# Halo matmuls paired inside a pair of chunks instead of with the pair before, in a four-image convolution kernel

## The chip, the cores and the metric

One core of a Trainium2 chip. The metric is device microseconds of one launch; a kernel before the change is run three times, and the median is given. One further execution was taken by the hardware profiler; all rows below are of that one. PE is TensorE's matmul part, DVE VectorE, ACT ScalarE, POOL GpSimd, SP the sync engine, which here only issues DMAs.

## The reference

```python
x = x + conv3x3(group_norm(x), L0_weight) + L0_bias
x = x + conv3x3(group_norm(x), L1_weight) + L1_bias
x = x + experts(group_norm(x))    # 8 experts: gelu(x w1 + b1) w2 + b2
x = x + conv3x3(group_norm(x), L3_weight) + L3_bias
```

x is (4, 8, 256, 256) in float32. A group is two of the eight channels of one image, so an image has to be complete before its next layer can be normalised. The experts are matrices over the width (256 to 1024 to 256), one per channel.

## The kernel before, in words

x stays in SBUF through all layers. A partition holds one of 8 channels, one of 8 neighbouring rows and one of the two columns of a column pair; an image is 32 x 128 = 4096 columns in 8 chunks of 512 (`CH`). A convolution layer is four steps, one per image: steps 0 to 3 are L0, 4 to 7 are L1, 8 to 11 are L3, with the experts between 7 and 8. A step treats its chunks in four pairs; "(g, k)" is pair k of step g.

Every number is used as a sum of two float16 parts, high and low, and three products of parts are accumulated (`PRODUCTS`). A step's way through the engines:
- statistics: DVE's `stats_chunk` per chunk (L586) and `aggregate` (L591); PE's `group_mean` (L807) and `group_variance` (L812), between them DVE's `deviation` and after them `variance`; GpSimd's `scale_and_bias` (L344 to L351) gives `norm_ok`.
- normalised input: ACT writes the high part in XN (L448) and the full value in SCR (L454), two buffers of two chunks; GpSimd subtracts (L365, `low_part`). In step 0 the full value is made by DVE instead (`first_whole`, L651, in PRE) and ACT writes only high parts.
- halos: rows above and below lie in other partitions. SP copies them by DMA from XN to HALO (L256), eight DMAs for the first half of the image (`halo_a`, after the third low part, or in step 0 the fourth) and eight for the second (`halo_b`).
- PE, per chunk, in one PSUM bank: three 128x128 matmuls (`centre`, L833), three times two 64x64 ones (`sides`, L840 and L842: the neighbouring columns), three times two 49x64 ones (`halo`, L852 and L854: rows and bias). The two of `sides` and the two of `halo` take the four quarters of the array, and run at once if they belong to different chunks. `sides` and `halo` of the same chunk write the same bank, and are kept apart by a wait.
- DVE adds the bank to x (`conv_update`, L624) and takes the next statistics from it (L586); in steps 8 to 11 there are no next statistics.

The order around the change is written out by hand in each engine's block. `tiles(pair, behind)` issues the sides of pair k beside the halos of pair k-1. So the first call of steps 0 and 8 has sides alone, a last call after steps 7 and 11 halos alone, and a pair is complete one call after its sides. PE waits for `halo_a` or `halo_b` before a call with halos of that half, and for `side_mm`, which a pair's last sides raised one call earlier. Five PSUM banks serve as a ring (`RING`): the centre of chunk q waits for the update of chunk q-5. GpSimd's list of `low_parts`, `scale_and_bias` and `pre_chunk` (input of the experts, transposed by PE, L892, split by ACT and DVE, L478 and L633) is a fixed sequence; `PREPARED` gives the steps in which transposes are made. In steps 0 and 1 PE and DVE also take the statistics of images 1 to 3 and of step 0's result in between.

SP's queue is in order: x (image 0 in four pieces), the ones (bias rows of HALO), the halos of steps 0 to 7, the expert weights, the halos of steps 8 to 11. Before the halos of step 10 and again before those of step 11 it waits for the image of step 8, or of step 9, and stores it (2 MB); image 2 and the eight chunks of image 3 are stored behind the halos of step 11.

## Time and profile before

| what | us |
|---|---|
| three runs | 606.98, 607.93, 610.66 (median 607.93) |
| the profiled execution, its own time | 608.81 |
| its span (first to last instruction) | 607.0 |
| PE busy in the span | 532.9 |
| DVE, ACT, POOL busy | 382.4, 266.7, 159.5 |
| experts in PE's timeline, about | 169 to 530 |

Busy PE is the time in which a matmul is in flight; back to back they overlap, so it is not PE at its peak. The stretches matter more than the totals: steps 0 to 7 lie before 169 us, steps 8 to 11 after 540 us. Statistics of the idle time name the instruction that came last before the engine went on.

### The profile page before, as it was taken

The numbers are of one execution on the slowest core, as the hardware profiler recorded it, in microseconds if no ns is written. First come the engines' busy times: TensorE is split into PE (matmuls) and PEld (weight loads), VectorE is DVE, ScalarE is ACT, GpSimd is POOL, SyncE is SP. The second block draws the span as 40 slices with busy tenths as digits, with TensorE's granted clock in tenths as the row PEclk, the third lists the DMA queues.
The fourth block names the chain that finished last, engine by engine and source line by source line (L and its number), as shares of the span: only waits on it lengthen the run. The fifth ranks groups of instructions, "written<-read, shape, count | busy, mean of one in ns | idle before, by whom it ended". The sixth has DMA issues, their size and how long they took to land.

```text
span 607.0 us, 9074 instructions
## 1 busy us (share of the span) xinstructions
PE 532.9 (88%) x3312; PEld 252.0 (42%) x3312; DVE 382.4 (63%) x658; ACT 266.7 (44%) x311; POOL 159.5 (26%) x168
## 2 busy tenths in 40 slices
PE   1565697999888999999999999999999997878984
PEld 0321242445454544444444444444444454544431
DVE  4996485999987549339158085193491638788533
ACT  0366348772353545336145163352461543665510
POOL 3744366997436000000000000000000000566520
PEclk9997797999979999999999999999999998979998
DMA  8724035554231022110120111011100000034678
GB/s 338 284 75 102 26 88 137 127 141 107 75 129 70 1 70 70 70 30 39 69 69 9 60 69 69 0 69 69 65 4 1 0 1 1 23 82 104 209 246 305
DMA packets 12293, 53.18 MB, mean 88 GB/s; under 512 B 2908, under 2 KB 3036, under 8 KB 9308
## 3 DMA queue, kind: packets, MB, share of 16 engines
q1 hardware_dynamic: 11976, 52.22, 26.7%
q10 hardware_dynamic: 288, 0.57, 0.3%
q8 instruction: 19, 0.31, 0.2%
q14 instruction: 10, 0.08, 0.0%
HBM read 25.83 MB, written 8.39 MB: 56 GB/s over the span
## 4 chain that ended last, share of the span: by engine, by line
PE 63%; DVE 21%; POOL 6%; SPq 3%; issue 2%; DMA 2%; ACT 1%; POOLq 0%; ACTq 0%; DVEq 0%
PE PS L952 27%; PE PS L931 25%; DVE ST L586 9%; PE PS L833 4%; POOL XN L365 4%; DVE X L624 4%; PE PS L840 3%; SPq L256 3%; DVE X L640 2%; DVE XT L633 2%; DVE PRE L651 1%; PE PS L908 1%; DMA X<-x 1%; PE PS L892 1%; DVE HID L724 1%
## 5 line engine op out<-in xcount | busy, mean ns | idle before, releaser
L931 PE MATMUL PS<-XT,W1S 128*128 (+1 forms) x768 | 171.8, 382 | 3.9 <-DVE W1S L647 3.7
L952 PE MATMUL PS<-HID,W2S 128*128 128x512 f16 x768 | 171.0, 380 | 1.6 <-DVE W2S L647 1.6
L486 ACT ACTIVATE SCR<-PS,CONST 128x512 f32<-128x512 f32 x128 | 87.3, 688 | 73.2 <-PE PS L931 37.1
L931 PEld LDWEIGHTS PS<-XT,W1S 128*128 128x128 f16 x768 | 75.5, 99 | 93.1 <-issue 7.0
L952 PEld LDWEIGHTS PS<-HID,W2S 128*128 128x128 f16 x768 | 75.4, 99 | 88.5 <-issue 2.4
L724 DVE SCALAR_TENSOR_TENSOR HID<-SCR,HID 128x512 f16<-128x512 f32 x128 | 88.5, 691 | 14.1 <-ACT HID L507 10.0
L365 POOL TENSOR_TENSOR XN<-SCR,XN 128x1024 f16<-128x1024 f32 x44 | 90.4, 2070 | 18.9 <-ACT SCR L454 18.6
L586 DVE BATCH_NORM_STATS2 ST<-X 128x6 f32<-128x512 f32 x128 | 86.3, 690 | 10.7 <-DMA X<-x 7.3
L647 DVE SCALAR_TENSOR_TENSOR W2S<-W2F,W2S 128x2048 f16<-128x2048 f32 x8 | 18.3, 2292 | 118.6 <-ACT W2S L482 118.6
L448 ACT ACTIVATE XN<-X,SC 128x1024 f16<-128x1024 f32 (+1 forms) x49 | 59.1, 1214 | 75.0 <-POOL SC L351 75.0
L624 DVE SCALAR_TENSOR_TENSOR X<-PS,X 128x512 f32<-128x512 f32 x96 | 64.9, 679 | 42.1 <-PE PS L854 41.7
L833 PE MATMUL PS<-XN,CWT 128*128 128x512 f16 x288 | 78.3, 408 | 12.7 <-DMA HALO<-ones 7.3
L333 POOL MEMSET HALO<- 48x520 f16 x12 | 6.3, 526 | 311.8 <-PE PS L931 311.2
L840 PE MATMUL PS<-XN,CWT 64*64 64x512 f16 x288 | 74.8, 395 | 5.6 <-DMA HALO<-XN 5.6
L842 PE MATMUL PS<-XN,CWT 64*64 64x512 f16 x288 | 74.8, 395 | 0.0
L852 PE MATMUL PS<-HALO,CWT 49*64 49x512 f16 (+1 forms) x288 | 73.5, 388 | 0.2 <-PE PS L842 0.2
L854 PE MATMUL PS<-HALO,CWT 49*64 49x512 f16 (+1 forms) x288 | 73.5, 388 | 0.0
L521 ACT ACTIVATE YT<-PS,CONST 128x512 f32 (+1 forms) x32 | 22.0, 687 | 114.0 <-PE PS L952 114.0
L454 ACT ACTIVATE SCR<-X,SC 128x1024 f32<-128x1024 f32 x44 | 54.0, 1228 | 15.6 <-POOL XN L365 15.6
L721 DVE TENSOR_SCALAR HID<-SCR 128x512 f16<-128x512 f32 x120 | 50.7, 422 | 8.5 <-ACT SCR L486 4.9
L833 PEld LDWEIGHTS PS<-XN,CWT 128*128 128x128 f16 x288 | 27.1, 106 | 51.3 <-issue 22.8
L840 PEld LDWEIGHTS PS<-XN,CWT 64*64 64x64 f16 x288 | 28.1, 111 | 47.1 <-issue 22.7
(43 smaller groups left out, 401.5 us busy)
## 6 DMA issues: line engine op xcount, KB each, us to landing
W1F<-w SPq DMA_DIRECT2D x8, 1024.0 KB, 4.8
W2F<-w SPq DMA_DIRECT2D x8, 1024.0 KB, 4.8
HALO<-XN SPq DMA_DIRECT2D x48, 129.9 KB
out<-X SPq DMA_DIRECT2D x3, 2048.0 KB, 7.0
HALO<-XN SPq DMA_DIRECT2D x48, 121.8 KB
X<-x SPq DMA_DIRECT2D x2, 2048.0 KB, 18.9
HALO<-XN SPq DMA_DIRECT2D x48, 64.9 KB
HALO<-XN SPq DMA_DIRECT2D x48, 60.9 KB
```

What stands on the lines that cost most here:

```text
L365: pool.tensor_tensor(XN[s][:, 1, rows, 1:NJ + 1], whole, XN[s][:, 0, rows, 1:NJ + 1], ALU.subtract).then_inc(lo_ok, 1)
L486: act.activation(SCR[:, ft % 2, 0:CH], bank(ft % G_RING), ACT.Gelu, bias=BT[:, ds(e * FT + ft, 1)], scale=1.0 / (XS * WS)).then_inc(gelu_o ...
L586: dve.bn_stats(ST[:, n % 4, slot], src).then_inc(bn_ok, 1)
L624: dve.scalar_tensor_tensor(out=xc, in0=bank(conv_bank(q)), scalar=1.0 / (XS * WS), in1=xc, op0=ALU.mult, op1=ALU.add).then_inc(x_new, 1)
L724: dve.scalar_tensor_tensor(out=HID[p][:, 1, ft], in0=SCR[:, ft % 2, 0:CH], scalar=HS, in1=HID[p][:, 0, ft], op0=ALU.mult, op1=ALU.subtract ...
L833: pe.matmul(to, CWT[:, w, l, 0:P], XN[s][:, part, rows, 1:NJ + 1], start=(n == 0), stop=False)
L840: odd = pe.matmul(bank(k, HALF_P, P), CWT[0:HALF_P, w, l, SIDE:EDGE], XN[s][0:HALF_P, part, rows, 2:NJ + 2], start=False, stop=False)
L842: even = pe.matmul(bank(k, 0, HALF_P), CWT[HALF_P:P, w, l, SIDE:EDGE], XN[s][HALF_P:P, part, rows, 0:NJ], start=False, stop=False)
L852: even = pe.matmul(bank(k, 0, HALF_P), CWT[0:kh, w, l, EDGE:CWN], HALO[s][0:kh, part, rows, 0:NJ], start=False, stop=last)
L854: odd = pe.matmul(bank(k, HALF_P, P), CWT[HALF_P:HALF_P + kh, w, l, EDGE:CWN], HALO[s][HALF_P:HALF_P + kh, part, rows, 0:NJ], start=False, ...
L931: mm = pe.matmul(bank(ft % G_RING), W1S[:, w, h * NF + ft * P:h * NF + (ft + 1) * P], rhs, start=(n == 0), stop=(n == 3 * DH - 1))
L952: mm = pe.matmul(bank(G2_BANK + h), W2S[:, w, ft * NW + h * P:ft * NW + (h + 1) * P], HID[p][:, part, ft], start=(ft == 0 and part == 0 an ...
```

## The change

Eight edits, all in the order of the work; the arithmetic stays.
1. `tiles(g, k)` treats one pair (a, b): sides of a beside halos of b, then a wait for all four of the last matmuls (`cross_mm`), then sides of b beside halos of a. There is no call with sides or halos alone. Both chunks of a pair end together, and `conv_update` waits for both. PE waits for the pair's halos at once.
2. Step 0's full-precision copy moves from DVE to ACT, by way of SCR, as in other steps.
3. GpSimd's list becomes regular: all low parts of a step but the last, then the next `scale_and_bias`, then the last; `pre_chunk` 0 comes behind all low parts of step 7.
4. Stores of images 0 to 2 leave SP's queue for ACT's, in halves: image 0 after the second and fourth normalised piece of step 11, images 1 and 2 behind that. SP keeps the eight chunks of image 3.
5. Image 0 is loaded in pieces of 3, 2, 2 and 1 chunks instead of four times two.
6. `deviation` and `variance` of steps 2 to 7 come one pair later on DVE; on PE, statistics 2 one pair earlier.
7. XT's low parts are made by DVE behind the pair of the same number instead of one pair earlier.
8. A slot of XN is free when the whole step has been computed (`conv_mm`), not when its sides have.

```diff
+X0_CUTS = (0, 3, 5, 7, 8)
...
 for _g in range(8, 12):
     for _k in range(NPR):
...
-        if (_g, _k) != (8, 0):
-            _q = NCH * _g + 2 * _k - 2
-            ORDER += [("c", _q // NCH, _q % NCH), ("c", _q // NCH, _q % NCH + 1)]
-ORDER += [("c", 11, NCH - 2), ("c", 11, NCH - 1)]
+        ORDER += [("c", _g, 2 * _k), ("c", _g, 2 * _k + 1)]
...
-            load_image(0, k * NT // 4, (k + 1) * NT // 4, x0_in[k])
+            load_image(0, TC * X0_CUTS[k], TC * X0_CUTS[k + 1], x0_in[k])
...
             halos(g)
-            if g >= 9:
-                sp.wait_ge(x_new, X_NEW_AT["c", g - 1, NCH - 1])
-                store_image(g - 9, 0, NT)
...
         def pre_chunk(m):
-            if m == 0:
-                pool.wait_ge(lo_ok, FIRST_PIECE[1])
...
-        low_parts(0)
-        scale_and_bias(1)
-        low_parts(1, 0, 3)
-        scale_and_bias(2)
-        low_parts(1, 3)
-        low_parts(2, 0, 2)
-        scale_and_bias(3)
-        low_parts(2, 2)
-        scale_and_bias(4)
-        low_parts(3)
...
-        scale_and_bias(8)
-        pre_chunk(0)
-        pre_chunk(1)
-        low_parts(7, 3)
-        for j in range(2, NCH):
+        for g in range(8):
+            low_parts(g, 0, -1)
+            scale_and_bias(g + 1)
+            low_parts(g, -1)
+        for j in range(NCH):
             pre_chunk(j)
...
-            if g > 0:
-                if m >= FIRST_PIECE[1] + 2:
-                    act.wait_ge(lo_ok, m - 1)
-                act.activation(SCR[:, m % 2, 0:n * CH], src, ACT.Identity,
+            if m >= 2:
+                act.wait_ge(lo_ok, m - 1)
+            act.activation(SCR[:, m % 2, 0:n * CH], src, ACT.Identity,
...
-                act.wait_ge(side_mm, 2 * NPR * (f + 1))
+                act.wait_ge(conv_mm, 2 * NCH * (f + 1))
...
+        def store_half(b, i):
+            act.wait_ge(x_new, X_NEW_AT["c", 8 + b, i + NCH // 2 - 1])
+            act.dma_start(out[b][:, i * CH:(i + NCH // 2) * CH], x_chunk(b, i, NCH // 2)
+                          ).then_inc(out_done, 16)
...
+        slot_free(11)
+        for k in range(NPR):
+            normalise_piece(FIRST_PIECE[11] + k)
+            if k % 2:
+                store_half(0, NPR * (k // 2))
+        for b in range(1, NB - 1):
+            for i in range(0, NCH, NCH // 2):
+                store_half(b, i)
...
-            dve.wait_ge(conv_mm, 2 * (q + 1))
+            dve.wait_ge(conv_mm, 4 * (q // 2 + 1))
...
-        dve.wait_ge(norm_ok, 1)
-        for i in range(NCH):
-            first_whole(i)
...
-                if i == 1 and g >= 2:
+                if i == 3 and g >= 2:
                     deviation(3 + g)
-                if i == 3 and g >= 2:
+                if i == 5 and g >= 2:
                     variance(3 + g)
-
-                after = (g, (i + 1) // 2) if i < NCH - 1 else (g + 1, 0)
-                if i % 2 and after in PREPARED:
-                    for m in PREPARED[after]:
+                if i % 2 and (g, i // 2) in PREPARED:
+                    for m in PREPARED[g, i // 2]:
                         xt_low(m)
...
+        def tiles(g, k):
+            a, b = 2 * k, 2 * k + 1
+            arrived = halo_a if 2 * k < SPLIT else halo_b
+            pe.wait_ge(arrived[SLOT[g]], HALO_HALF * (USES[g] + 1))
+            for n, (part, w) in enumerate(PRODUCTS):
+                first = cross_mm if n == 2 else None
+                sides(g, a, part, w, first)
+                halo(g, b, part, w, first)
+
+            pe.wait_ge(cross_mm, 4 * (NPR * g + k + 1))
+            for n, (part, w) in enumerate(PRODUCTS):
+                second = conv_mm if n == 2 else None
+                sides(g, b, part, w, second)
+                halo(g, a, part, w, second)
...
-                q = NPR * g + k - 1
-                tiles((g, k), (q // NPR, q % NPR) if q >= 0 else None)
+                tiles(g, k)
+                if g == 0 and k == 1:
+                    group_mean(2)
                 if g == 0 and k == 2:
-                    group_mean(2)
-                if g == 0 and k == 3:
                     group_variance(2)
...
-        tiles(None, (7, NPR - 1))
```

## Rows read from the trace of the kernel before

**Rows 1.** Busy time by stretch: us of each engine (instructions), granted clock, DMA share, GB/s.
```profile
112.00:137.00 25.00, 23.99 (x244) 10.38 (x240) 24.23 (x47) 20.52 (x19) 24.12 (x21) 1.00 0.53 133
...
565.00:607.00 42.00, 32.35 (x341) 13.06 (x339) 17.03 (x29) 9.17 (x8) 9.65 (x8) 0.96 0.78 275
```

**Rows 2.** Timeline of PE, 25 to 27 us: start, us, what [idle before, releaser].
```profile
25.75 1.86 PE L833 MATMUL PS<-XN,CWT 128*128 128x512 f16 x4 [7.34 <-DMA HALO<-ones]
```

**Rows 3.** Timeline of VectorE, 16 to 27 us.
```profile
17.40 8.94 DVE L651 TENSOR_SCALAR PRE<-X,SC 128x512 f32<-128x512 f32 x8 [0.90 <-POOL SC L351]
```

**Rows 4.** Timeline of VectorE, 30 to 46 us.
```profile
32.55 0.14 DVE L597 TENSOR_TENSOR SM<-MV,PS 128x1 f32<-128x1 f32 x1
...
37.04 0.63 DVE L624 SCALAR_TENSOR_TENSOR X<-PS,X 128x512 f32<-128x512 f32 x1
```

**Rows 5.** Timeline of PE, 47 to 58 us.
```profile
53.47 0.59 PE L807 MATMUL PS<-MV,CONST 128*128 128x1 f32 x2 [5.05 <-DVE MV L591]
```

**Rows 6.** Timeline of VectorE, 57 to 81 us.
```profile
58.08 0.69 DVE L624 SCALAR_TENSOR_TENSOR X<-PS,X 128x512 f32<-128x512 f32 x1 [4.43 <-PE PS L854]
...
72.38 0.69 DVE L624 SCALAR_TENSOR_TENSOR X<-PS,X 128x512 f32<-128x512 f32 x1 [4.14 <-PE PS L854]
...
80.90 0.37 DVE L591 BATCH_NORM_AGGREGATE MV<-ST 128x2 f32<-128x48 f32 x1
```

**Rows 7.** Timeline of PE, 94 to 100 us.
```profile
96.15 0.63 PE L840 MATMUL PS<-XN,CWT 64*64 64x512 f16 x1 [3.68 <-DMA HALO<-XN]
```

**Rows 8.** Timeline of GpSimd, 77 to 97 us.
```profile
81.07 0.55 POOL L344 TENSOR_TENSOR RS<-SM,RS 128x1 f32<-128x1 f32 x1 [7.06 <-DVE SM L609]
```

**Rows 9.** Timeline of SP's queue, 530 to 607 us: start, us, DMA issues.
```profile
580.34 14.22 SPq L256 DMA_DIRECT2D HALO<-XN  x16
594.60 9.56 SPq L240 DMA_DIRECT2D out<-X  x9
```

**Rows 10.** Chain that ended last, 580 to 607 us: start, us, what.
```profile
580.99 1.38 SPq L256
...
587.32 0.62 SPq L256
...
593.93 2.36 DMA HALO<-XN
...
598.88 1.34 DVE X L624 x2
```

**Rows 11.** Timeline of PE, 584 to 588.5 us.
```profile
584.26 1.49 PE L833 MATMUL PS<-XN,CWT 128*128 128x512 f16 x6
...
587.11 1.49 PE L833 MATMUL PS<-XN,CWT 128*128 128x512 f16 x6
```

**Rows 12.** Timeline of PE, 597 to 600 us.
```profile
597.45 0.38 PE L852 MATMUL PS<-HALO,CWT 49*64 49x512 f16 x1
...
598.00 0.37 PE L852 MATMUL PS<-HALO,CWT 49*64 49x512 f16 x1 [0.17 <-PE PS L842]
...
598.21 0.38 PE L852 MATMUL PS<-HALO,CWT 48*64 48x512 f16 x1
```

**Rows 13.** Page, part 5: costliest groups (x count, busy us, mean ns, idle before, releaser).
```profile
L365 POOL TENSOR_TENSOR XN<-SCR,XN 128x1024 f16<-128x1024 f32 x44 | 90.4, 2070 | 18.9 <-ACT SCR L454 18.6
...
L454 ACT ACTIVATE SCR<-X,SC 128x1024 f32<-128x1024 f32 x44 | 54.0, 1228 | 15.6 <-POOL XN L365 15.6
```

**Rows 14.** Timeline of PE, 164 to 170 us.
```profile
168.81 1.44 PE L931 MATMUL PS<-XT,W1S 128*128 128x512 f16 x3 [3.73 <-DVE W1S L647]
```

**Rows 15.** Timeline of VectorE, 164 to 175 us.
```profile
166.42 2.28 DVE L647 SCALAR_TENSOR_TENSOR W1S<-W1F,W1S 128x2048 f16<-128x2048 f32 x1
...
171.39 0.37 DVE L591 BATCH_NORM_AGGREGATE MV<-ST 128x2 f32<-128x48 f32 x1
```

**Rows 16.** Timeline of GpSimd, 565 to 582 us.
```profile
569.71 0.19 POOL L351 TENSOR_TENSOR SC<-SM,SC 128x1 f32<-128x1 f32 x1
```

**Rows 17.** Page, part 6: DMA issues: x count, KB each, median us to landing.
```profile
out<-X SPq DMA_DIRECT2D x3, 2048.0 KB, 7.0
```

More of the change, by code:

```diff
@@ L356, in low_part @@
             s = SLOT[g]
+            pool.wait_ge(xn_ok, m + 1)
             pool.wait_ge(hi_ok, m + 1)
-            if g == 0:
-                pool.wait_ge(whole0_ok, i + n)
-                whole = whole0[:, i:i + n].rearrange("p c (t j) -> p (c t) j", j=NJ)
-            else:
-                pool.wait_ge(xn_ok, m + 1 - FIRST_PIECE[1])
-                whole = SCR[:, m % 2, 0:n * CH].rearrange("p (t j) -> p t j", j=NJ)
             rows = slice(i * TC, (i + n) * TC)
-            pool.tensor_tensor(XN[s][:, 1, rows, 1:NJ + 1], whole,
+            pool.tensor_tensor(XN[s][:, 1, rows, 1:NJ + 1],
+                               SCR[:, m % 2, 0:n * CH].rearrange("p (t j) -> p t j", j=NJ),
                                XN[s][:, 0, rows, 1:NJ + 1], ALU.subtract).then_inc(lo_ok, 1)
@@ L577, in _ @@
         normalise_piece(FIRST_PIECE[8] + 3)
-        for g in range(9, 12):
-            normalise(g)
+        def store_half(b, i):
+            act.wait_ge(x_new, X_NEW_AT["c", 8 + b, i + NCH // 2 - 1])
+            act.dma_start(out[b][:, i * CH:(i + NCH // 2) * CH], x_chunk(b, i, NCH // 2)
+                          ).then_inc(out_done, 16)
+        for g in range(9, 11):
+            normalise(g)
+        slot_free(11)
[6 more added lines that the diff above has]
+                store_half(b, i)
     @block.vector
@@ L613, in input_stats @@
             if b == 0:
-                dve.wait_ge(x0_in[i // 2], 16)
+                if i in X0_CUTS:
+                    dve.wait_ge(x0_in[X0_CUTS.index(i)], 16)
             elif b == 1:
@@ L834, in centre, with sides, halo @@
                           start=(n == 0), stop=False)
-        def sides(g, i, part, w, last):
+        def sides(g, i, part, w, signal=None):
             s, l, k = SLOT[g], g // 4, conv_bank(NCH * g + i)
-            rows = slice(i * TC, (i + 1) * TC)
+            rows, last = slice(i * TC, (i + 1) * TC), signal is conv_mm
             odd = pe.matmul(bank(k, HALF_P, P), CWT[0:HALF_P, w, l, SIDE:EDGE],
-                            XN[s][0:HALF_P, part, rows, 2:NJ + 2], start=False, stop=False)
+                            XN[s][0:HALF_P, part, rows, 2:NJ + 2], start=False, stop=last)
             even = pe.matmul(bank(k, 0, HALF_P), CWT[HALF_P:P, w, l, SIDE:EDGE],
-                             XN[s][HALF_P:P, part, rows, 0:NJ], start=False, stop=False)
-            if last:
-                even.then_inc(side_mm, 1)
-                odd.then_inc(side_mm, 1)
-        def halo(g, i, part, w, last):
+                             XN[s][HALF_P:P, part, rows, 0:NJ], start=False, stop=last)
+            if signal is not None:
+                even.then_inc(signal, 1)
+                odd.then_inc(signal, 1)
+        def halo(g, i, part, w, signal=None):
             s, l, k = SLOT[g], g // 4, conv_bank(NCH * g + i)
-            rows, kh = slice(i * TC, (i + 1) * TC), KH if part == 0 else HK
+            rows, last = slice(i * TC, (i + 1) * TC), signal is conv_mm
+            kh = KH if part == 0 else HK
             even = pe.matmul(bank(k, 0, HALF_P), CWT[0:kh, w, l, EDGE:CWN],
@@ L856, in halo @@
                             start=False, stop=last)
-            if last:
-                even.then_inc(conv_mm, 1)
-                odd.then_inc(conv_mm, 1)
-        def tiles(pair, behind):
-            for c in range(2):
-                if behind is not None and c == 0:
-                    g, k = behind
-                    arrived = halo_a if 2 * k < SPLIT else halo_b
-                    pe.wait_ge(arrived[SLOT[g]], HALO_HALF * (USES[g] + 1))
-                    pe.wait_ge(side_mm, 2 * (NPR * g + k + 1))
-                for n, (part, w) in enumerate(PRODUCTS):
-                    if pair is not None:
-                        g, k = pair
-                        sides(g, 2 * k + c, part, w, n == 2 and c == 1)
-                    if behind is not None:
-                        g, k = behind
-                        halo(g, 2 * k + c, part, w, n == 2)
+            if signal is not None:
+                even.then_inc(signal, 1)
+                odd.then_inc(signal, 1)
+        def tiles(g, k):
[11 more added lines that the diff above has]
+                halo(g, a, part, w, second)
         def before_step(g):
@@ L1068, in _ @@
                     group_variance(15)
-                q = NPR * (g - 8) + k - 1
-                tiles((g, k), (8 + q // NPR, q % NPR) if q >= 0 else None)
-        tiles(None, (11, NPR - 1))
+                tiles(g, k)
     ctx.close()
```

32 lines of the change are left out of this document (6 added, 26 removed).

## The prediction, made before the changed kernel was run

> **What bounds the kernel now.** The busy time by stretch comes first. Between 112 and 137 us PE is busy for 23.99 of 25 us and VectorE for 24.23, at full clock: steps 4 and 5 are a tie. From 565 us PE has 32.35 of 42 us, with DMA busy for 0.78 of it [rows 1]. Experts (169 to 530 us) aren't touched. So three places can move: the front, the pace of the conv steps, and the tail.
>
> The front: PE's first matmul waits until 25.75 for the ones, which lie in SP's queue behind all of x [rows 2]. VectorE meanwhile makes step 0's full-precision copy for 8.94 us [rows 3]. It reads mean 1 at 32.55 and starts its first update at 37.04 [rows 4]. In step 1 PE and VectorE alternate instead of overlapping: PE idles 5.05 us for statistics 3 [rows 5], VectorE 4.43 and 4.14 us for PE (and 4.20 and 2.62 in the same view), 15.4 us in all; step 1 ends at 81.27 [rows 6]. In step 3 PE waits 3.68 us for a halo and restarts at the lower clock [rows 7]; the cause is GpSimd, which stood 7.06 us at scale 4, with step 3's low parts behind it [rows 8].
>
> The tail: SP issues step 11's halo copies from 580.34 to 594.56, and only then image 2's store and image 3's eight chunks, nine issues in 9.56 us [rows 9]. The chain runs through these copies, a landing of 2.36 us, PE and two updates [rows 10].
>
> All starts are of the profiled execution: span 607.0, time 608.81, so 1.8 us lie around it; the median of the three runs is 607.93, 0.88 below.
>
> **Part 1: the pairing.** A pair costs six centre and six side/halo starts: centres begin at 584.26 and again at 587.11, a pitch of 2.85 us [rows 11]. The new tiles have the same six starts, but PE must see the first three finish before the fourth. This drain exists once now, in the tail: a start at 597.45, the next at 598.00 [rows 12], 0.55 apart, against 0.21 to the one after that. That is 0.34 more; four signals rather than two are awaited, so I take 0.36 a pair (below: 0.15, if the array drains anyway at each change from centres to tiles; above: 0.5). A pair becomes 3.21 us, a step with its two statistics (0.2 each) 13.2 us. VectorE needs 12.2 with its waits in steps 4 and 5, so PE becomes the bound. Behind the wait stand the second half, the next centres and statistics; VectorE waits for all of it, and now gets both chunks at once.
> The Trainium skill (TensorE: Matmul & The Clock Gate, The cost: per-tile semaphore tail) says that increments on tiles serialize, 26.3 ns each; by it two more awaited cost 0.05 us a pair, an estimate from that page, 1.8 us over the 35 drains that matter.
>
> **Part 2: nothing lags.** No sides go in front and no halos behind: 1.5 us less of PE at 163.6 and at 598.0, but there the gain is given back: at the end VectorE's two updates (1.34 us, [rows 10]) no longer overlap the last halos. In step 1 VectorE has pair (1,0) complete before it ends step 0, so the alternation goes. The cost is that tiles (0,0), hence everything behind it on PE, now waits for halo_a(0).
>
> **Part 3: the front, step by step.** The copies move from VectorE to ScalarE. Norm 0 still comes at 17.4 (three chunks land first, at about 7.5, and eight stats then take until 12.4 as now). A copy takes ScalarE 1.23 us per two chunks and its other pass as much, GpSimd's low part takes 2.07 [rows 13]; ScalarE paces, with a piece every 2.27 us in its timeline. The fourth low part ends at 27.1 (26.0 now), SP issues eight halos of 0.65 us until 32.4, they land 2.4 after the last issue starts: tiles (0,0) run 34.4 to 37.3, at the lower clock (1.2 GHz, as after the idle time in [rows 7], where starts are 0.43 apart) since PE idles six us before. Centres to 39.0, then mean 1. VectorE, which freed 8.9 us, stands at deviation 1 from about 23 until 39.4 and its gain is lost. Norm 1 comes at 43.0, and the first update at 44.1, 7.1 us late.
> GpSimd now does step 0's last low part behind scale 1: 45.1; its eight halos land at 52.2; tiles (0,2) end at 55.1, where VectorE (at 52.2) waits 2.9. Step 0's statistics end at 63.7 (53.6 now). Scale 2, then low part (1,3), then halos: 70.0, so tiles (1,2) end at 71.8 (VectorE waits 2.1). Step 1 ends at 78.3, and tiles (2,0) at 78.7, against 81.5 now for the same work: **2.8 us ahead**, because 15.4 us of alternation shrink to some 2.
>
> **Part 4: steps 2 to 7.** Scale 4 no longer stands in front of step 3's first three low parts: 80.4, halos landed at 87.4, needed at 90.2. So [rows 7] goes: 3.7 idle plus about 2.6 at the lower clock, 6.3 us. Next late would be GpSimd, at 4 x 2.27 + 1.9 = 11.0 a step, under 13.2. From (2,1) to (7,3) are 23 drains: +8.3. Pre chunk 0 now comes behind all of step 7's low parts, PE waits 1.3 for it (0.6 now); a second small wait (0.65) goes, with 1.0 of transposes in front of the last halos and 0.7 of other gaps. The deviations and variances come one pair later (3 us); cover: step 4's halos land at 98.0 and are needed at 103.3, later steps have as much, and without it each us late stands on PE. The wait for a free slot on the whole step instead of its sides ends at the same matmuls. Sum: 83.6 us now (81.5 to 165.1) - 6.3 + 8.3 + 0.7 - 2.35 = 84.0. Tiles (7,3) end at about 162.8.
> At present W1's low part stands in front of the last two updates, and PE starts the experts at 168.81 [rows 14], while VectorE still updates until 171.6 [rows 15]. After the change the last updates (2.65) and two XT parts (1.2) come between: W1 ends at 164.8, 167.5, 168.7. The experts start at 168.7: **0.1 us earlier**. Three gains of 2.8, 6.3 and 3.1 us end in nothing, by the drains and this order.
>
> **Part 5: tail.** In step 8 VectorE need not wait as now at the ring: tiles (9,0) end at 563.7 with pair (9,0) complete, 3.5 us ahead. Norm 15 depends on (9,3)'s update and comes at 570.8 (569.9 now, [rows 16]). Seven pairs of 3.21 and one statistic later, (11,0) could start at 588.3. SP, without stores, starts halos 11 at 580.0 rather than 580.34: the low parts bind, not SP. Eight issues at 0.65 (if nothing slows them; 1.38 and 0.62 both stand in [rows 10]) and the landing give 587.6, and the second half 592.9 for a need at 594.7.
> Stores now go from ScalarE: image 0 in halves after pieces 1 and 3 of step 11 (the issue, some 0.4 us, moves pieces 2 and 3 and the low parts behind them), image 1 at once behind, image 2 at 582 and 588. So some 5 MB are in flight from 580 on, beside the halos. A store of 2 MB takes 7.0 us [rows 17], so the backlog lasts to about 598. For both together I allow the halos 1.2 us (bounds: 0.4, the issue alone, and rival 1). PE ends at 600.8 (599.5 now), the updates at 602.1 (600.2), the last store is issued at once rather than behind eight others, and lands about 2.9 later (3.6 for the last now, behind a full queue), 605.0; the exit 0.4. Span 605.4, less the 0.1: **605.3**, 1.7 us less than 607.0. The time is 607.1 for that execution, 606.2 for the median.
> The Trainium skill (DMA: Bandwidth & Descriptors, Issuing engines are not separate DMA queues) says that DMAs of all engines share the same 16 engines, so issuing from another one saves only the issuing time. By it the move saves SP's nine issues and not the contention; the 4 slow issues in [rows 10] agree that a store slows halos, but no row here has the store on another queue.
>
> **Rivals.** 1 (slower): ScalarE's stores hold up halos 11. Now a store of 2 MB makes four of the copies behind it last 1.38 instead of 0.62. With 5 MB in flight some 14 of 16 would: the second half lands at 580.0 + 14 x 1.42 + 1.3 + 2.4 = 603.6, then two pairs less a centre run (4.9), updates 1.3, store 3.3: span 613.1, time 614.0. It decides from the fifth slow copy on. For it: [rows 10]. Against it: they shared one queue, and PE in step 10 didn't wait. 0.17.
> 2 (faster): the drain is mostly there already, 0.15 a pair. 35 x 0.21 = 7.4 us less (a step is then 12.4, still over VectorE's 12.2): 598.8. For it: 12 x 0.21 is 2.55, so the pitch of 2.85 already holds 0.3 for its two changes of shape [rows 11, 12]. Against it: [rows 12], where the same mechanism shows its 0.55. 0.18.
> 3: the waits at the front don't add as worked out: mean 1 late by 7 us pushes statistics 2 and 3 and all behind them, and halos in steps 2 and 3 come late again. 3 to 5 us more, 610. 0.15. In itself within 1%.
> Forecast: 0.50.
>
> **Numbers.** A measurement tells from no change about 1%, 6.1 us: below 601.9 faster, above 614.0 slower. Slower has most of rival 1 and the end of rival 3: 0.17. Faster has rival 2 and little else: 0.18. The rest 0.65. The range reaches to rival 2's 598.8 and to rival 1's 614.0; it leaves out 0.2.
>
> **Signs.** Right, if the first update stands at about 44, VectorE's alternation in step 1 shrinks to under 4 us, no halo wait stands at step 3, the pitch of a pair is 3.2 us, halos 11 are issued in about 10.5 us, and one or two stores follow the last update. Wrong, if the pitch is under 3.05 or over 3.35, if many copies of step 11 last 1.3 or more, or if the first update starts before 40.

## The result, and the profile after

The changed kernel takes 615.00 us (median of 4 runs, 614.41 to 615.68) against 608.64 us for the kernel before in the same comparison: a ratio of 1.0103 with a 95% interval of 1.0069 to 1.0138. It is slower by 1.0%, where 606.2 us was forecast, with 614.0 as the upper end. The profiled execution took 614.91 us with a span of 613.1, against a forecast span of 605.3.

First the page of the kernel after: span, busy time by engine, DMA by fortieth of the span, one group and one row of DMA issues.

```profile
span 613.1 us, 9025 instructions
...
PE 536.8 (88%) x3312; PEld 245.7 (40%) x3312; DVE 372.7 (61%) x650; ACT 271.3 (44%) x316; POOL 159.2 (26%) x168
...
DMA  8613455542211021110111021102100000224784
...
L806 PE MATMUL PS<-XN,CWT 64*64 64x512 f16 x288 | 83.8, 399 | 27.4 <-DMA HALO<-XN 20.3
...
out<-X ACTq DMA_DIRECT2D x6, 1024.0 KB, 7.1
```

Of the 27.4 us for which PE stands in front of tiles, 20.3 are put down to halo copies. Three waits make up most of them: 5.08 and 5.58 us in step 0, and one of 9.01 in the tail. The busy time by stretch shows that one from above (the columns are those of [rows 1]):

```profile
565.00:579.00 14.00, 13.28 (x141) 4.53 (x144) 5.29 (x10) 8.93 (x8) 7.43 (x7) 1.00 0.64 207
579.00:593.00 14.00, 8.04 (x78) 2.62 (x70) 3.87 (x6) 0.24 (x1) 2.19 (x2) 0.99 0.99 369
593.00:599.00 6.00, 2.51 (x24) 0.74 (x24) 0.00 (x0) 0.00 (x0) 0.00 (x0) 0.50 0.60 175
599.00:613.00 14.00, 9.66 (x98) 3.11 (x90) 5.16 (x8) 0.00 (x0) 0.00 (x0) 0.98 0.42 154
```

To 579 us PE is busy for 13.28 of 14 us. From 579 to 593 it has 8.04 of 14, and the DMA engines are busy for 0.99 of the time at 369 GB/s: that stretch belongs to them. The third row has a granted clock of 0.50, so PE restarts at 1.2 GHz. The chain of waits names what stood in front (start, us, what):

```profile
579.64 0.16 SPq L247
...
579.85 1.38 SPq L247
581.27 1.40 SPq L247
582.71 2.06 SPq L247
584.80 1.96 SPq L247
586.80 2.14 SPq L247
588.98 2.28 SPq L247
591.31 4.99 DMA HALO<-XN
...
596.34 0.63 PE PS L806
```

L247 is SP issuing step 11's halo copies. The second to the eighth last 1.38 to 2.28 us (1.41 the eighth, which began at 591.31), and the copies land at 596.30, 4.99 us after the last of them was begun. In the kernel before, four copies of 1.37 to 1.40 us stand behind the store [rows 10], the others take 0.59 to 0.63 but for one of 1.32 at 591.90, and the landing takes 2.36. On ScalarE's queue stand the stores beside which they ran (start, us, engine, line, operation):

```profile
576.88 1.82 ACTq L545 DMA_DIRECT2D out<-X  x3
...
580.98 6.72 ACTq L545 DMA_DIRECT2D out<-X  x2
```

A first half image had gone at 570.08 and landed at 574.93. Three more (3 MB) are issued at 576.88, 577.27 and 577.76, a further one at 580.98 and the last at 587.36. The one of 577.76 lands at 588.44 and the one of 580.98 at 591.74, 10.7 and 10.8 us after their issue, where a whole image took 7.0 [rows 17]. So five half images, 5 MB, are under way at some time beside the copies, but never more than 3 MB of them at once.

PE's timeline in the kernel after: where it begins the experts, one pair of step 9 and the next centres, and the restart in the tail:

```profile
169.60 1.01 PE L897 MATMUL PS<-XT,W1S 128*128 128x512 f16 x2 [5.01 <-DVE XT L612]
...
566.71 1.49 PE L799 MATMUL PS<-XN,CWT 128*128 128x512 f16 x6
568.13 0.40 PE L806 MATMUL PS<-XN,CWT 64*64 64x512 f16 x1
...
569.12 0.40 PE L806 MATMUL PS<-XN,CWT 64*64 64x512 f16 x1
...
569.90 1.49 PE L799 MATMUL PS<-XN,CWT 128*128 128x512 f16 x6
...
596.34 0.63 PE L806 MATMUL PS<-XN,CWT 64*64 64x512 f16 x1 [9.01 <-DMA HALO<-XN]
```

Centres to centres is 569.90 - 566.71 = 3.19 us (2.85 in [rows 11]). The drain, PE's wait until the first half of a pair's tiles is finished, lies between the two groups: the first group's third starts come at 568.59, the next group's first at 569.12, 0.53 later against 0.21 inside a group. PE starts the experts at 169.60, where [rows 14] have 168.81. Around 203 us the two kernels stand level again (203.02 and 203.11), so the front gave and took nothing on balance. VectorE at the front:

```profile
37.99 0.15 DVE L575 TENSOR_TENSOR SM<-MV,PS 128x1 f32<-128x1 f32 x1 [16.23 <-PE PS L773]
...
42.49 0.63 DVE L603 SCALAR_TENSOR_TENSOR X<-PS,X 128x512 f32<-128x512 f32 x1
```

It stands 16.23 us at deviation 1 and makes its first update at 42.49 (37.04 in [rows 4]).

### The profile page after: what moved, and what is told of

It is laid out like the page before. It is cut to its first block, busy times and chain, and to the rows that moved or that the text cites. A ratio compares the mean times of both kernels' runs of the same rounds, so it can differ in the third digit from the quotient of the medians.

```text
span 613.1 us, 9025 instructions
## 1 busy us (share of the span) xinstructions
PE 536.8 (88%) x3312; PEld 245.7 (40%) x3312; DVE 372.7 (61%) x650; ACT 271.3 (44%) x316; POOL 159.2 (26%) x168
## 4 chain that ended last, share of the span: by engine, by line
PE 73%; DVE 11%; SPq 4%; POOL 3%; DMA 3%; ACT 3%; issue 2%; DVEq 0%; POOLq 0%; ACTq 0%
PE PS L918 27%; PE PS L897 25%; PE PS L806 9%; PE PS L799 7%; DVE ST L564 4%; SPq L247 4%; DMA HALO<-XN 2%; DVE X L603 2%; DVE X L619 2%; PE PS L858 2%; PE PS L874 1%; POOL XN L349 1%; DMA X<-x 1%; ACT XN L413 1%; ACT SCR L418 1%
## 5 line engine op out<-in xcount | busy, mean ns | idle before, releaser
L450 ACT ACTIVATE SCR<-PS,CONST 128x512 f32<-128x512 f32 x128 | 87.2, 687 | 72.4 <-PE PS L897 36.3
L806 PE MATMUL PS<-XN,CWT 64*64 64x512 f16 x288 | 83.8, 399 | 27.4 <-DMA HALO<-XN 20.3
L349 POOL TENSOR_TENSOR XN<-SCR,XN 128x1024 f16<-128x1024 f32 (+1 forms) x49 | 99.4, 2030 | 25.1 <-ACT SCR L418 25.1
L819 PE MATMUL PS<-HALO,CWT 49*64 49x512 f16 (+1 forms) x288 | 84.2, 400 | 0.0
L821 PE MATMUL PS<-HALO,CWT 49*64 49x512 f16 (+1 forms) x288 | 84.2, 400 | 0.0
L808 PE MATMUL PS<-XN,CWT 64*64 64x512 f16 x288 | 83.8, 399 | 0.0
L799 PE MATMUL PS<-XN,CWT 128*128 128x512 f16 x288 | 75.1, 399 | 8.1 <-DMA HALO<-ones 8.1
L418 ACT ACTIVATE SCR<-X,SC 128x1024 f32<-128x1024 f32 (+1 forms) x49 | 59.3, 1210 | 0.0
L806 PEld LDWEIGHTS PS<-XN,CWT 64*64 64x64 f16 x288 | 23.8, 108 | 81.9 <-PE PS L821 31.5
L799 PEld LDWEIGHTS PS<-XN,CWT 128*128 128x128 f16 x288 | 27.1, 105 | 45.1 <-issue 22.7
```

The lines of the kernel that those rows point to most:

```text
L349: pool.tensor_tensor(XN[s][:, 1, rows, 1:NJ + 1], SCR[:, m % 2, 0:n * CH].rearrange("p (t j) -> p t j", j=NJ), XN[s][:, 0, rows, 1:NJ + 1] ...
L450: act.activation(SCR[:, ft % 2, 0:CH], bank(ft % G_RING), ACT.Gelu, bias=BT[:, ds(e * FT + ft, 1)], scale=1.0 / (XS * WS)).then_inc(gelu_o ...
L799: pe.matmul(to, CWT[:, w, l, 0:P], XN[s][:, part, rows, 1:NJ + 1], start=(n == 0), stop=False)
L806: odd = pe.matmul(bank(k, HALF_P, P), CWT[0:HALF_P, w, l, SIDE:EDGE], XN[s][0:HALF_P, part, rows, 2:NJ + 2], start=False, stop=last)
L808: even = pe.matmul(bank(k, 0, HALF_P), CWT[HALF_P:P, w, l, SIDE:EDGE], XN[s][HALF_P:P, part, rows, 0:NJ], start=False, stop=last)
L819: even = pe.matmul(bank(k, 0, HALF_P), CWT[0:kh, w, l, EDGE:CWN], HALO[s][0:kh, part, rows, 0:NJ], start=False, stop=last)
```

## The experiments

All ratios are against the kernel before, on the same chip. The kernel after was timed only in the first comparison, where the kernel before had 608.64 us; in the three later ones it had 607.83 to 608.10. Differences to the 615.00 us therefore cross two comparisons. My theory after the result: the bytes of the stores that are in flight beside step 11's halo copies cost the time, and the rest of the change is neutral. Rivals: the drains cost it and the stores only show it; ScalarE's queue is what hurts, not the bytes; the late start of the front costs it.

**e1: after, with images 0 to 2 stored by SP behind step g's halos again.**

```diff
             halos(g)
+            if g >= 9:
+                sp.wait_ge(x_new, X_NEW_AT["c", g - 1, NCH - 1])
+                sp.dma_start(out[g - 9], x_chunk(g - 9, 0, NCH)).then_inc(out_done, 16)
...
-        for g in range(9, 11):
+        for g in range(9, 12):
             normalise(g)
-        slot_free(11)
-        for k in range(NPR):
-            normalise_piece(FIRST_PIECE[11] + k)
-            if k % 2:
-                store_half(0, NPR * (k // 2))
-        for b in range(1, NB - 1):
-            for i in range(0, NCH, NCH // 2):
-                store_half(b, i)
```

> The changed kernel with one part undone: images 0 to 2 are stored from SP's queue again, as before the change (each whole, after the halos of the next step but one). Theory S (ScalarE's stores slow the halo copies of step 11, PE waits 9.0 us for them): the wait before tiles (11,0) shrinks to under 4 us, at most five of the sixteen copies last over 1 us, and the time is 606 to 609 us, against 615.0. Theory D (the drains alone are the loss): the copies don't matter to the end, 614 to 615 us.

Measured: 607.21 us, ratio 0.9987 (0.9970 to 1.0005), span 605.5. Every copy of step 11 lasts 0.59 to 0.69 us, the second half's issues end at 591.5, no wait stands at tiles (11,0), and the last update ends at 601.8. The busy time of the stretch in which the kernel after stood:

```profile
579.00:593.00 14.00, 13.41 (x135) 4.38 (x132) 5.65 (x9) 1.97 (x2) 3.92 (x2) 1.00 0.72 232
```

PE has 13.41 of 14 us instead of 8.04. So 7.8 us of the kernel after (7.1 by the two ratios, 7.6 by the spans) are the stores' place alone, and everything else that the change does comes to no measurable difference. (Its last update ends 1.6 us later than in the kernel before, and 3.7 us of the span are left behind it instead of 6.8.) Image 1's store went out at 576.67 and landed at 583.60, and the copies, from 580.94, were not slowed by the rest of it: a store begun 4.3 us ahead of them cost nothing, where the one begun 0.6 us ahead (579.72, kernel before) cost four slow copies.

**e2: before, with only the stores moved to ScalarE in halves**, as the kernel after has them.

```diff
             halos(g)
-            if g >= 9:
-                sp.wait_ge(x_new, X_NEW_AT["c", g - 1, NCH - 1])
-                store_image(g - 9, 0, NT)
...
-        for g in range(9, 12):
+        for g in range(9, 11):
             normalise(g)
+        slot_free(11)
+        for k in range(NPR):
+            normalise_piece(FIRST_PIECE[11] + k)
+            if k % 2:
+                store_half(0, NPR * (k // 2))
+        for b in range(1, NB - 1):
+            for i in range(0, NCH, NCH // 2):
+                store_half(b, i)
```

> The kernel before with the changed kernel's stores of images 0 to 2 on ScalarE's queue, all else as before. Theory S: step 11's copies slow down here too (six or more over 1.3 us), the first half lands at about 596 rather than 590.5, and since PE needs it one pair later and has 2 us of slack at the end of the queue, the time rises by only 1 to 3 us over the kernel before. Rival: the slow copies belong to the new pairing's timing; then SP's freed queue makes this kernel 2 to 4 us faster than before.

Measured: 611.47 us, ratio 1.0055 (1.0037 to 1.0073), span 609.2. Seven copies of step 11 last 1.19 to 2.49 us, and PE waits 7.87 us at 595.3. PE's timeline has it:

```profile
595.29 0.63 PE L850 MATMUL PS<-XN,CWT 64*64 64x512 f16 x1 [7.87 <-DMA HALO<-XN]
```

It is the same wait in the other order of the work, so it belongs to the stores and not to the pairing. The last update ends at 606.7, 6.5 us later than in the kernel before (600.2). The time grows by only 3.4 (1 to 3 were expected), since the move also gives something back: of the old span 6.8 us lie behind the last update, where SP's nine issues stand [rows 9], and here 2.5.

**e3: before, with the drain alone**, a wait for the first half of each group of sides and halos.

```diff
+    half_mm = sem("half_mm")
...
+                if c == 1 and pair is not None:
+                    g, k = pair
+                    pe.wait_ge(half_mm, 2 * (NPR * g + k + 1))
                 for n, (part, w) in enumerate(PRODUCTS):
...
-                        sides(g, 2 * k + c, part, w, n == 2 and c == 1)
+                        sides(g, 2 * k + c, part, w, n == 2 and c == 1,
+                              half_mm if n == 2 and c == 0 else None)
```

> The kernel before with a drain added in the middle of each pair's tiles (PE waits for the third group's side matmuls before it starts the fourth), same matmuls in the same order. Theory D: pitch of a pair 3.19 instead of 2.85 us in steps 4 and 5, the experts start 4 to 6 us later, the whole is 5 to 9 us slower. Rival (VectorE's 12.2 us a step covers it): under 2 us slower.

Measured: 607.89 us, ratio 1.0004 (0.9977 to 1.0031). A miss: 5 to 9 us were expected and none came. The drain is there, in PE's timeline:

```profile
106.67 0.40 PE L841 MATMUL PS<-XN,CWT 64*64 64x512 f16 x1
...
107.59 0.40 PE L841 MATMUL PS<-XN,CWT 64*64 64x512 f16 x1
...
108.37 1.49 PE L834 MATMUL PS<-XN,CWT 128*128 128x512 f16 x6
109.79 0.40 PE L841 MATMUL PS<-XN,CWT 64*64 64x512 f16 x1
```

A pair takes 109.79 - 106.67 = 3.12 us, 0.27 over [rows 11]. But where PE then waits for something else, the drain is paid out of that wait: the halo wait of step 3 is 2.86 instead of 3.68, and step 3 ends at 109.7 instead of 110.9. In the tail a wait of 1.89 us at 590.5 is gone too. Steps 4 and 5, the tie of [rows 1], do lengthen (12.9 and 13.2 us against 12.2 and 11.9), and the experts start 0.7 us later, at 169.5. A cost per pair times the number of pairs is an upper bound on the end time, not an estimate of it.

**e4: after, with mean and variance 1 ahead of tiles (0,0).**

```diff
-                if (g, k) == (0, 1):
+                if (g, k) == (0, 0):
                     group_mean(1)
                     group_variance(1)
```

> The changed kernel with mean 1 and variance 1 issued on PE ahead of tiles (0,0) instead of behind them. Theory F (VectorE's 16 us wait at deviation 1, 21.8 to 38.0, throws away what it gained in the front): VectorE's first update stands at 36 to 37 instead of 42.5, halo_b(0) no longer waits for norm 1, tiles (2,0) start at 66 to 68 instead of 76.1, and the experts start some 9 us earlier: 605 to 608 us. Rival (another wait takes over, as GpSimd's order or statistics 3 and 4): 611 to 615.

Measured: 608.1 us, ratio 0.9994 (0.9977 to 1.0011), 6.9 us under the kernel after (6.6 by the ratios). VectorE at the front:

```profile
28.40 0.15 DVE L575 TENSOR_TENSOR SM<-MV,PS 128x1 f32<-128x1 f32 x1 [6.58 <-PE PS L773]
...
36.59 0.69 DVE L603 SCALAR_TENSOR_TENSOR X<-PS,X 128x512 f32<-128x512 f32 x1 [3.60 <-PE PS L821]
```

The wait shrinks from 16.23 to 6.58 us and the first update comes at 36.59, 5.9 us sooner. PE starts the experts at 161.6, 8.0 us sooner than in the kernel after. Then the tail takes some back: eight slow copies, and PE waits 9.33 us at 588.9. So the front's late start is real and costs 8 us at the experts. Since the two kernels stand level around 203 us all the same, the rest of the new order must have earned as much. PE starts the experts 8 us sooner here where some 9 were expected.

**e5: after, ScalarE's half stores kept apart from step 11's copies**: image 0 ahead of step 11's pieces, image 1 at 571.7 and 576.2, image 2 when halo_b of step 11 has landed.

```diff
+        store_half(0, 0)
+        store_half(0, NPR)
         slot_free(11)
+        store_half(1, 0)
         for k in range(NPR):
             normalise_piece(FIRST_PIECE[11] + k)
-            if k % 2:
-                store_half(0, NPR * (k // 2))
...
+            if k == 1:
+                store_half(1, NPR)
+        act.wait_ge(halo_b[SLOT[11]], HALO_HALF * (USES[11] + 1))
+        store_half(2, 0)
+        store_half(2, NPR)
```

> The changed kernel, still with six half stores on ScalarE's queue, but placed apart from the halos of step 11: image 0 after step 10's pieces (about 562), image 1 before piece 0 and after piece 1 of step 11 (570 and 575), image 2 only when the second half of step 11's halos has landed. Theory S: the first copies of step 11 are issued at 0.62 us but for two or three behind image 1, PE's wait before (11,0) is under 3 us, 605 to 609 us. If the queue that issues is what slows the copies and not the bytes in flight, 5 or more stay over 1 us and the time stays at 612 or more.

Measured: 608.90 us, ratio 1.0011 (0.9996 to 1.0026). There is one slow copy (1.29 us), no wait at tiles (11,0), and the last update ends at 601.8. With the same queue and the same sizes at other times the loss is gone. It is the overlap that costs, not the issuing engine.

**e6: after, with the next pair's centres between the two halves of the tiles**, to fill the drain.

```diff
...
-                tiles(g, k)
+                tiles_first(g, k)
+                centres(g, k + 1)
...
+                tiles_second(g, k)
```

> The changed kernel with the same pairing, but the centres of the next pair stand between the two halves of a pair's tiles, so that PE has 1.4 us of work while the first half finishes. Theory D: the 0.55 us between the two halves goes, pitch 2.85 to 2.95 us, VectorE's 12.2 us bind steps 2 to 5, experts start 4 to 6 us earlier; step 11 still waits for its halos, so only that carries to the end: 609 to 612 us. If the ring of five banks holds the centres (they need the update of the pair that has just ended), pitch stays over 3.1 and the time at 614 to 616.

Measured: 624.64 us, ratio 1.0271 (1.0245 to 1.0296). A miss, and a large one: 9.6 us slower than the kernel after. The drain is gone from PE's timeline: in step 10, which has no statistics and no wait, a step takes 11.4 us (4 x 2.85) where the kernel after has 12.8. But elsewhere the time isn't: the second half of a pair now comes behind the next pair's centres, so VectorE gets both chunks later, and PE waits for VectorE at the statistics. One such place, VectorE's timeline:

```profile
116.87 0.14 DVE L575 TENSOR_TENSOR SM<-MV,PS 128x1 f32<-128x1 f32 x1
...
117.11 1.44 DVE L579 SCALAR_TENSOR_TENSOR SM<-SM,MV 128x1 f32<-128x1 f32 x1
...
122.09 0.69 DVE L603 SCALAR_TENSOR_TENSOR X<-PS,X 128x512 f32<-128x512 f32 x1 [0.77 <-PE PS L821]
```

and PE's waits (in total, times, longest):

```profile
PE PS L806 <- DMA HALO<-XN: 23.8, 4, 11.9
...
PE PS L778 <- DVE SM L579: 10.6, 9, 1.9
```

In the kernel after the second sum is 5.5. By the ends of the steps, step 1 takes 20.1 us (14.8 in the kernel after) and step 2 16.6 (13.7); steps 3 and 4 give 2.0 back, and step 5 takes 13.6 in both. The experts start at 174.8 instead of 169.6, 5.2 us later; by the end of step 10 it is 8.0 (595.3, not 587.3), and PE's wait for step 11's halos is 11.9 us instead of 9.0. That the later second half is what starts the waits is argued from these rows; no run has it by itself.

**e7: after, with images 0 to 2 held until step 11's last halo has landed.**

```diff
...
-        slot_free(11)
...
+        act.wait_ge(halo_b[SLOT[11]], HALO_HALF * (USES[11] + 1))
-        for b in range(1, NB - 1):
+        for b in range(NB - 1):
             for i in range(0, NCH, NCH // 2):
                 store_half(b, i)
```

> The changed kernel with all stores of images 0 to 2 held until the last halo copy of step 11 has landed. A measurement of the copies without any store: theory S says all sixteen last 0.59 to 0.64 us from 579.2 on, the first half lands at about 587, PE doesn't wait at (11,0), and PE ends at 600 instead of 609. The end is then bound by 8 MB of stores from about 593 on: span 611 to 616. If the copies are slow for another reason, PE's wait stays.

Measured: 618.49 us, ratio 1.0167 (1.0145 to 1.0189). The copies last 0.59 to 0.63 us but for one of 1.03, PE doesn't wait and the last update ends at 602.4 (601.8 in e1). But then the stores are what is left:

```profile
585.00:600.00 15.00, 14.38 (x140) 4.83 (x138) 6.44 (x10) 0.00 (x0) 0.00 (x0) 1.00 0.76 258
600.00:616.00 16.00, 0.85 (x12) 0.26 (x12) 1.29 (x2) 0.00 (x0) 0.00 (x0) 0.60 0.90 361
```

Sixteen microseconds at 361 GB/s with PE done. The stores must be early or in between; both ends cost.

**e8: e4's, e5's and e6's edits together**, with mean and variance 1 in front of step 0's first tiles.

```diff
...
+        centres(0, 0)
+        group_mean(1)
+        group_variance(1)
...
+                tiles_first(g, k)
+                centres(g, k + 1)
+                tiles_second(g, k)
...
+        act.wait_ge(halo_b[SLOT[11]], HALO_HALF * (USES[11] + 1))
+        store_half(2, 0)
+        store_half(2, NPR)
```

> The changed kernel with the three edits together: mean 1 and variance 1 ahead of tiles (0,0), next centres between the halves, stores apart from the halos. If the three causes are separate, the gains add: 615 less 9 (front), 5 (drains before the experts), 8 (stores), 3 (drains in the tail), 588 to 596 us, faster than both kernels. If one hides behind another, 600 or more.

Measured: 605.03 us (603.10 to 609.38, a wide scatter), ratio 0.9963 (0.9934 to 0.9992). Again a miss: e6's order, which I had expected to gain 8 us, takes back some 5 to 7 of what the two others give (compare e9 below, 598.00 without it). It starts the experts at 165.8 where e4 had 161.6, and 13.4 us of PE's waits are for deviations (5.5 in the kernel after). By this and e6 the drain is better left where it is in steps that have statistics; in step 10, which has none, filling it gains 1.4 us in both.

**e9: after, with e4's and e1's edits** (mean and variance 1 ahead of tiles (0,0); images 0 to 2 on SP).

```diff
-                if (g, k) == (0, 1):
+                if (g, k) == (0, 0):
...
+            if g >= 9:
+                sp.wait_ge(x_new, X_NEW_AT["c", g - 1, NCH - 1])
+                sp.dma_start(out[g - 9], x_chunk(g - 9, 0, NCH)).then_inc(out_done, 16)
...
```

> The changed kernel with two edits: mean 1 and variance 1 ahead of tiles (0,0), as in e4, and the stores of images 0 to 2 back on SP's queue, as in e1. If both costs are separate: experts start at 161.6 as in e4, step 10 ends at 580, no wait over 3 us before (11,0), and 599 to 602 us, faster than both kernels by 1%. If the front's gain is lost again in the tail: 605 or more.

Measured: **598.00 us** (597.76 to 598.61, 5 runs), ratio 0.9837 (0.9824 to 0.9850). It beats both kernels, the one before by 1.6%. The stretches of the tail:

```profile
565.00:579.00 14.00, 13.42 (x136) 4.56 (x129) 5.76 (x9) 6.59 (x6) 8.15 (x4) 1.00 0.73 247
579.00:593.00 14.00, 11.44 (x118) 3.72 (x115) 5.83 (x10) 0.00 (x0) 0.00 (x0) 1.00 0.87 315
```

No wait stands at tiles (11,0), PE is busy until its work ends (the last update ends at 592.4), the experts start at 161.6, no copy lasts over 1 us. What e4 gains at the front, 8 us, arrives at the end in full once the tail doesn't give it back (607.2 in e1, 598.0 here). The time is 1 us below the 599 to 602 expected.

**e10: after, with only image 1 (2 MB) beside step 11's copies, still on ScalarE's queue.**

```diff
...
+        store_half(0, 0)
+        store_half(0, NPR)
+        normalise(11)
+        store_half(1, 0)
+        store_half(1, NPR)
+        act.wait_ge(halo_b[SLOT[11]], HALO_HALF * (USES[11] + 1))
+        store_half(2, 0)
+        store_half(2, NPR)
```

> The changed kernel with only 2 MB (image 1) on ScalarE's queue beside the first halo copies of step 11, at the same moment as in the changed kernel (577); image 0 goes at 562, image 2 after the last halo has landed. Theory S-bytes (the copies wait for the bytes in flight, whatever the queue): four, at most five copies over 1 us, as with 2 MB on SP's queue in the kernel before; PE waits 2 to 4 us before (11,0); 607 to 610 us. Theory S-queue (a second queue is what hurts): seven copies slow as in the changed kernel, 613 or more.

Measured: 609.16 us, ratio 1.0026 (1.0003 to 1.0048). Its chain of waits:

```profile
580.37 1.39 SPq L247
...
581.80 1.44 SPq L247
...
583.29 1.18 SPq L247
...
584.51 1.06 SPq L247
...
585.61 0.59 SPq L247
...
586.91 2.43 DMA HALO<-XN
```

There are four slow copies, as many as the kernel before has behind an image on SP's own queue, and the landing is back at 2.43 us. PE waits 1.51 us, less than the 2 to 4 expected.

**e11: after, all stores on SP, with images 0 and 1 (4 MB) right ahead of step 11's copies.**

```diff
+            if g == 11:
+                sp.wait_ge(x_new, X_NEW_AT["c", 9, NCH - 1])
+                sp.wait_ge(lo_ok, PIECE_OF[11, SPLIT] + 1)
+                for b in range(2):
+                    sp.dma_start(out[b], x_chunk(b, 0, NCH)).then_inc(out_done, 16)
             halos(g)
...
```

> The changed kernel with all stores on SP's queue, but images 0 and 1 (4 MB) directly ahead of step 11's halo copies and image 2 behind them. Theory S-bytes: seven or eight copies over 1 us and PE waits 7 to 10 us before (11,0), as with ScalarE's stores; 613 to 617 us. Theory S-queue: no more than five slow copies, PE waits under 5 us, 610 or less.

Measured: 617.42 us, ratio 1.0162 (1.0142 to 1.0181). From its chain of waits:

```profile
582.90 2.27 SPq L247
...
585.22 1.39 SPq L247
...
592.46 1.89 SPq L247
...
594.39 3.62 DMA HALO<-XN
```

There are seven slow copies and a wait of 8.04 us at 598.1, with nothing at all on ScalarE's queue. e10 and e11 settle it for the number of slow copies: 2 MB begun within 2.4 us of the first copy make four, and 4 MB or more make seven (eight in e4), on either queue. The single copy is not the same: five of e11's seven take 1.36 to 1.52 us, with 4 MB under way at once on SP's queue, where the kernel after has up to 2.28 with at most 3 MB at once on ScalarE's. From the first copy's start to the eighth's it is 11.5 us here and 12.1 there, so the sums are close. The slow copies end about when the stores land: 586.65 and 586.68 in the kernel before, 594.35 and 594.75 here, 585.57 and 584.85 in e10.

**e12: before, with GpSimd in the regular order of the kernel after for steps 1 to 6.**

```diff
-        low_parts(1, 0, 3)
-        scale_and_bias(2)
-        low_parts(1, 3)
...
+        for g in range(1, 7):
+            low_parts(g, 0, 3)
+            scale_and_bias(g + 1)
+            low_parts(g, 3)
```

> The kernel before with GpSimd's regular order of the changed kernel (scale g+1 behind the third low part of step g) for steps 1 to 6, else as before. If scale 4 in front of step 3's low parts was the cause of the 3.68 us wait for a halo at 96.2 us, that wait goes, the experts start 4 to 6 us earlier, and the time is 602 to 604 us. Rival (the pace of VectorE in steps 4 to 7 sets the experts' start anyway): the wait goes, but less than 1 us is won.

Measured: 605.10 us, ratio 0.9953 (0.9935 to 0.9972). The 3.68 us in front of step 3 [rows 7] are gone and step 3 takes 12.9 us instead of 18.4, but step 1 takes 2.2 us more and step 4 0.8 more. The experts start at 165.5, 3.4 us sooner, and the end is 3.0 us sooner, both a little short of what was expected. This part of the change is worth having by itself.

## Why the prediction was wrong

**The step that failed** is in Part 5: "For both together I allow the halos 1.2 us (bounds: 0.4, the issue alone, and rival 1)." The term for what the stores do to step 11's copies was mis-sized: the runs show 9.01 us of waiting there, and none with the stores elsewhere (e1, e5). The forecast span of 605.3 becomes 613.1 like this: tiles (11,0) were ready at 587.34 instead of 588.3 (-1.0), the wait is 9.0 instead of 1.2 (+7.8), the first pair after it runs at the lower clock, 596.34 to 599.48 against 568.13 to 569.90 (+1.4), and the last store lands 2.2 us after the last update instead of 2.9 (-0.7): +7.5 of 7.8.

How I came to so small a number can be seen in the working. I had the row that priced it: four slow copies behind 2 MB [rows 10]. I had the amount too, "some 5 MB". And I had the Trainium skill (DMA: Bandwidth & Descriptors, Issuing engines are not separate DMA queues), by which the queue makes no difference but for the issuing time; the numbers of slow copies in e10 and e11 agree with it, the time of the single copy depends on more. Instead of multiplying, I let "they shared one queue" stand as a reason against Rival 1. With the same engines behind both queues there was none. The forecast and Rival 1 should have changed places. Multiplying would still not have given the whole: eight first copies at 1.38 instead of 0.65 us put the halos at 593.4 and the wait at about 5 us, an estimate from the prediction's own terms. The rest of the 9.0 is that the copies took up to 2.28 us and the landing 4.99.

**Rival 1** had the mechanism, and its span of 613.1 is the measured one, but in part by luck. It had 14 copies at 1.42 us and PE held by the second half; by its own price, four copies for 2 MB, 5 MB make 10 and not 14. In fact seven copies last 1.38 to 2.28 us, the landing takes 4.99 instead of 2.4, PE is held by the first half, and the second is issued by 598.31, not 602. It also used the price of a copy behind 2 MB for all of them; in the kernel after the price was higher.

Point by point, the rest:

- *Part 1, the drain.* 3.21 us a pair forecast, 3.19 measured; 0.27 in e3 against 0.36. Rival 2 (0.15) is out. By the Trainium skill (TensorE: Matmul & The Clock Gate, The cost: per-tile semaphore tail) two more awaited increments would be 0.05 us, an estimate from that page; a drain costs 0.27 us where two are awaited (e3) and 0.34 where four are (3.19 - 2.85), so the increments are the small part of it.
- *Part 2, nothing lags.* VectorE's waits for PE in step 1 are 0.16, 1.14 and 0.30 us where they were 15.4 in all [rows 6].
- *Part 3, the front.* First update 42.49 (44.1 forecast), step 0's statistics 62.91 (63.7), step 1's 77.14 (78.3), tiles (2,0) end at 77.98 (78.7). All 0.7 to 1.6 early, mostly from one term: the fourth low part ends at 26.0 rather than 27.1, so tiles (0,0) start at 33.27 and not at 34.4. They take 3.1 us to the next centres (2.9 forecast), with starts 0.43 apart, the pace of the lower clock. "Its gain is lost" was right and is shown by e4: moved ahead, mean 1 gives 8.0 us at the experts. Rival 3 is out, because no part of the front came later than forecast.
- *Part 4.* Tiles (7,3) end at 163.56 (162.8); the experts start at 169.60 (168.7). No halo wait stands at step 3, as forecast, and e12 gives that part alone 3.4 us at the experts in the old order, of the 6.3 that I had; step 3 by itself gets 5.5 us shorter. One term wasn't foreseen: VectorE's deviation of 2.05 us at 110.61, for which PE waited 1.71 us (below).
- *Part 5, without the stores.* e1 ends its last update at 601.8 (602.1 forecast) with a span of 605.5 (605.3). That this is so close is in part luck: the 602.1 has the 1.2 us for the stores in it, which e1 doesn't pay, and e1 reaches the end of step 10 1.7 us later than the kernel after (589.1 against 587.3). The other steps held to within about 2 us.

Between the sizes of Part 4's terms and what they are worth at the end there is a gap that this case leaves partly open: e3 says that 23 drains cost the old order 0.7 us at the experts, while my sum has +8.3 for the new one. Both can be true, since the old order had other waits to pay them from and the new one had few; a kernel in the new order without drains and without e6's later results wasn't tried.

## What to carry to other kernels

Before a store is moved to another queue, ask what small, awaited copies will be in flight beside it, and price them by the bytes, as if it were the same queue: here 5 MB of stores, 3 MB of them begun 1.5 to 2.3 us ahead of eight copies that PE waits for, cost 7 to 8 us against e1. The same stores kept apart from the copies cost 1.7 against e1 (e5). A gain at the front is real only when the tail can take it; e4 and e9 differ by the stores alone, and by 10 us. And a per-pair cost times the number of pairs is an upper bound where the engine waits for something else anyway; so is the gain from filling such a gap, if the filling makes a result late.

## What the runs showed of the hardware that I had not expected

- The time that SP spends on issuing one halo copy grows beside stores that have just begun: 0.59 to 0.69 us (e1), 1.37 to 1.40 behind 2 MB on its own queue (kernel before), 1.06 to 1.44 beside 2 MB on ScalarE's (e10), 1.36 to 2.28 behind 4 MB on its own (e11), 1.38 to 2.28 in the kernel after. The landing behind the eighth copy grows too: 2.43 us in e10, 3.62 in e11, 4.99 in the kernel after. A store under way isn't enough by itself: in e1 the copies from 580.94 took 0.61 to 0.69 us while image 1 landed only at 583.60. And there are single slow copies beside no store of images 0 to 2 (1.03 us in e7, 1.32 at 591.90 in the kernel before). What sets the time of one copy stays open.
- A last store into idle DMA queues lands in 2.2 us (610.53 to 612.70), against 3.6 behind a full queue.
- A granted clock of 1.00 in a view can mean that nothing was recorded. Tiles (0,0), after 5.08 us without work, start 0.43 us apart, as tiles (11,0) do after 9.01 us; the view gives 1.00 for 33.2 to 36.3 us and 0.50 for 596.3 to 597.9. But the trace of the kernel after has no record of the clock before 36.34 us, and the view counts that as 1.00. In e4, where the record begins at 28.68, the same tiles start 0.43 us apart too, and the view has 0.50:

```profile
33.00:36.30 3.30, 2.83 (x24) 0.74 (x24) 0.00 (x0) 3.30 (x4) 2.83 (x2) 0.50 0.31 76
```

So read the pace from the starts, and look where the record begins.
- VectorE's small operation of line 579, 128 values with two inputs in SBUF, takes 0.22 us, but 2.05 at 110.61, where GpSimd's operation of 2.06 us had started 0.03 before:

```profile
110.61 2.05 DVE L579 SCALAR_TENSOR_TENSOR SM<-SM,MV 128x1 f32<-128x1 f32 x1
```

```profile
110.58 2.06 POOL L349 TENSOR_TENSOR XN<-SCR,XN 128x1024 f16<-128x1024 f32 x1 [0.20 <-ACT SCR L418]
```

Both end within 0.02 us of each other. In e6 the same line takes 1.33, 1.65, 2.02, 0.52, 1.44 and 1.45 us between 65 and 132 us, each time until GpSimd's operation ends. That is part of why its variances came late, for PE waits for exactly this result. It agrees with the Trainium skill (SBUF — State Buffer, SBUF: two separate sides), which says that a VectorE operation with two inputs in SBUF and a GpSimd operation that reads it exclude each other for the whole instruction. Whether a kernel gains from moving the deviation between two low parts wasn't tried.
